# Key factors turned once and spread over all rows by DMA, in a fused Perceiver layer

## The reference, cut to what matters

```python
x2 = layernorm(modality2, ln2_g, ln2_b)
k = x2 @ Wk + bk
scores = jnp.einsum('bqe,bke->bqk', q, k) * scaling
attn = jax.nn.softmax(scores, axis=-1)
```

## Time and profile before

| | us |
|---|---|
| three runs | 562.96, 566.79, 568.53 |
| median | 566.79 |
| the profiled execution | 566.35 |
| its span | 564.6 |
| TensorE busy (matmuls) | 525.6 (93%) |
| VectorE busy | 342.0 (61%) |
| ScalarE busy | 196.1 (35%) |
| GpSimd busy | 193.2 (34%) |
| ScalarE's DMA queue | 17,792 packets, 12.58 MB |
| SP's DMA queue | 24,256 packets, 109.20 MB |

### The profile page before, as it was taken

The page is one execution under the profiler, slowest core; times in us unless marked ns, Lnnn a source line. Parts: engine busy times, 40 slices in busy tenths (PEclk is TensorE's granted clock), DMA queues, the critical chain, the costliest instruction groups (busy, mean ns, idle before and its releaser), DMA issues.

```text
span 564.6 us, 10435 instructions
## 1 busy us (share of the span) xinstructions
PE 525.6 (93%) x4171; PEld 301.9 (53%) x4171; DVE 342.0 (61%) x765; ACT 196.1 (35%) x455; POOL 193.2 (34%) x132
## 2 busy tenths in 40 slices
PE   4979988987999989999998999999988879999996
PEld 2834446553765845666484575656574334444442
DVE  6754185373768468377575836967596895435333
ACT  0233014433723541653373255145143542211110
POOL 0141213224316233440721524269364991000000
PEclk9989999998999999999999999999999989999999
DMA  8999895498499789959959986853527420002002
GB/s 278 424 375 423 330 357 217 184 343 274 174 390 245 276 301 236 324 204 367 262 208 391 202 330 227 241 184 154 113 75 192 145 74 1 1 0 75 0 2 75
DMA packets 42096, 122.45 MB, mean 217 GB/s; under 512 B 19640, under 2 KB 21432, under 8 KB 37312
## 3 DMA queue, kind: packets, MB, share of 16 engines
q1 hardware_dynamic: 24256, 109.20, 53.5%
q10 hardware_dynamic: 17792, 12.58, 9.6%
HBM read 111.29 MB, written 10.49 MB: 216 GB/s over the span
## 4 chain that ended last, share of the span: by engine, by line
PE 61%; DVE 11%; DMA 8%; issue 8%; POOL 5%; ACT 4%; SPq 2%; ACTq 0%; DVEq 0%; POOLq 0%
PE u_ps L914 11%; PE s_ps L1147 9%; PE w_ps L1132 8%; DMA area<-in_kt_dram 6%; PE s_ps L824 6%; PE u_ps L835 5%; PE w_ps L937 5%; POOL area L414 2%; PE w_ps L846 2%; PE w_ps L928 2%; DVE area L1241 2%; PE s_ps L1031 2%; DMA area<-in_nat_dram 2%; PE w_ps L900 1%; DVE area L1325 1%
## 5 line engine op out<-in xcount | busy, mean ns | idle before, releaser
L1241 DVE BATCH_NORM_STATS2 area<-area 128x6 f32<-128x384 f32 (+1 forms) x208 | 99.7, 546 | 26.8 <-DMA area<-in_nat_dram 26.8
L824 PE MATMUL s_ps<-area 128*64 128x512 f32 (+1 forms) x384 | 72.8, 522 | 5.8 <-DMA area<-in_kt_dram 4.8
L914 PE MATMUL u_ps<-area 128*64 128x384 f32 (+1 forms) x416 | 72.4, 491 | 1.2 <-DVE area L1301 1.2
L1147 PE MATMUL s_ps<-area 128*128 128x512 f16 x256 | 61.7, 385 | 4.8 <-DVE area L1520 4.8
L1132 PE MATMUL w_ps<-area 128*128 128x512 f16 x256 | 60.7, 378 | 0.2 <-ACT area L724 0.2
L449 POOL TENSOR_SCALAR area<-area 128x512 f16<-128x512 f32 x32 | 55.6, 1753 | 15.0 <-DMA area<-in_wf_dram 15.0
L414 POOL TENSOR_TENSOR area<-area 128x16 f32<-128x16 f32 (+1 forms) x16 | 39.0, 2438 | 46.6 <-DVE area L1256 46.6
L1283 DVE CUSTOM_DVE_ANT_0 area<-w_ps,area 128x512 f32<-128x512 f32 x24 | 15.4, 690 | 58.6 <-PE w_ps L797 51.8
L724 ACT ACTIVATE area<-w_ps,area 128x512 f32<-128x512 f32 x32 | 22.0, 686 | 79.5 <-PE w_ps L1132 74.0
L824 PEld LDWEIGHTS s_ps<-area 128*64 128x64 f32 x384 | 24.1, 139 | 44.9 <-issue 40.6
L914 PEld LDWEIGHTS u_ps<-area 128*64 128x64 f32 (+1 forms) x416 | 27.6, 135 | 34.2 <-issue 29.5
(11 more groups left out here) (169 smaller groups left out, 835.9 us busy)
## 6 DMA issues: line engine op xcount, KB each, us to landing
area<-in_nat_dram SPq DMA_DIRECT2D x48, 768.0 KB, 10.3
area<-in_kt_dram SPq DMA_DIRECT2D x24, 1536.0 KB, 7.8
area<-in_wf_dram SPq DMA_DIRECT2D x32, 256.0 KB, 8.2
skew<-area ACTq DMA_DIRECT2D x8, 1024.0 KB, 8.6
area<-in_wf_dram SPq DMA_DIRECT2D x16, 512.0 KB, 3.4
area<-in_aw_dram SPq DMA_DIRECT2D x4, 1024.0 KB, 9.3
area<-skew ACTq DMA_DIRECT2D x16, 256.0 KB, 12.2
area<-in_x_dram SPq DMA_DIRECT2D x8, 256.0 KB, 10.2
```

Source lines behind the costliest of these rows:

```text
L824: ins = pe.matmul(S[ch][u * L:(u + 1) * L, 0:n], a_sb[:, c, u * L:(u + 1) * L], x[:, u, c, :], start=(c == 0), stop=(c == KC - 1))
L914: ins = pe.matmul(U[u * L:(u + 1) * L, 0:DC], pT[g % 2][0:m, i, u * L:(u + 1) * L], nat[0:m, j, u, :], start=(j == 0), stop=(j == NJ - 1))
L1147: ins = pe.matmul(S[q], g[i % 3][:, q * P:(q + 1) * P], wf16[:, f, 1, :], start=(f == 0 and z == 0), stop=(f == KF - 1 and z == 1))
L1241: dve.bn_stats(st[b][0:m, 2 * j + u, :], nat[0:m, j, u, :]).then_inc(s["key_stats"], 1)
```

## The change

The factors are no longer spread by ScalarE and turned 13 times. `turn_factors` turns `rs` twice (128 x 13, once for each sequence of the pair) into free columns of `S[3]`; ScalarE copies the 13 x 256 result to SBUF and stores it in DRAM as 26 rows of 128 (13 KB); after a wait for the store it issues two loads, each of which brings one sequence's 13 rows (6,656 B) to 64 partitions. `spread` then holds in SBUF what `W[0]` to `W[2]` and `S[3]` held in PSUM, and `scale_scores` reads it there. `turn_factors(p + 1)` stands ahead of the last chunk of scores, `factors_out` behind `yT_out`, `factors_load` behind the last `scores_out`. `relative(t)` moves ahead of `turn_probs(p, 0)`, and some waits move from `key_factors` to its neighbours. On SP the loads of `wm` move behind those of `nat`, `x` and `kt`.

```diff
+        factor_rows, at = carve(at, [NJ, 2 * P])
...
-        spread, at = carve(at, [P, NJ, P])
+        spread, at = carve(at, [P, NJ * P])
...
+        factors = nc.dram_tensor("factors", (NI, P), F32, kind="Internal").ap()
...
@@ SP, step @@
                 for k in range(NG + 1):
                     if more:
                         load_nat(n + 1, k)
-                    if k in (1, 3, NG) and (1, 3, NG).index(k) + 2 < len(wms):
-                        load_wm(wms[(1, 3, NG).index(k) + 2])
+                for i in wms[2:4]:
+                    load_wm(i)
                 if n + 2 < NT:
                     load_x(n + 2)
                 if more and n:
                     load_kt(n + 1, 2)
-                if len(wms) > 5:
-                    load_wm(wms[5])
+                for i in wms[4:6]:
+                    load_wm(i)
...
@@ ScalarE @@
-            def spread_factors(p, g):
...
+            def factors_out(p):
+
+                act.wait_ge(s["factors_turned"], p + 1)
+                act.copy(factor_rows, S[3][0:NJ, 2 * P:4 * P]).then_inc(s["factors_taken"], 1)
+                act.wait_ge(s["factors_taken"], p + 1)
+                at_least(act, s["factors_spread"], 32 * p)
+                act.dma_start(factors.rearrange("(u j) k -> j u k", u=2), factor_rows.rearrange("j (u k) -> j u k", u=2)).then_inc(s["factors_stored"], 16)
+
+            def factors_load(p):
+
+                act.wait_ge(s["factors_stored"], 16 * (p + 1))
+                at_least(act, s["chunk_scaled"], 4 * p)
+                for u in range(2):
+                    act.dma_start(spread[u * L:(u + 1) * L, :], factors[u * NJ:(u + 1) * NJ, :].rearrange("j k -> (j k)").partition_broadcast(L)).then_inc(
+                        s["factors_spread"], 16)
...
-                if more:
-                    spread_factors(p + 1, 0)
-                    spread_factors(p + 1, 1)
                 if r is not None and more:
                     z_out(r)
...
                 yT_out(p)
                 if more:
+                    factors_out(p + 1)
                     scores_out(p + 1, ORDER[3])
-                    spread_factors(p + 1, 2)
-                    spread_factors(p + 1, 3)
+                    factors_load(p + 1)
                 for i in wms[4:6]:
                     magnitude(i)
...
@@ TensorE @@
-            def key_factors(p):
...
+            def turn_factors(p):
+
+                pe.wait_ge(s["rs_ready"], 2 * (p + 1))
+                pe.wait_ge(s["scores_taken"], 4 * p + PLACE[NCH] + 1)
+                for u in range(2):
+                    ins = pe.transpose(S[3][0:NJ, (2 + u) * P:(3 + u) * P], rs[p % 2].rearrange("p (j u) -> p u j", u=2)[:, u, :], ident_f)
+                ins.then_inc(s["factors_turned"], 1)
...
-            for ch in ORDER:
+            for ch in ORDER[0:3]:
                 scores(0, ch)
+            turn_factors(0)
+            scores(0, ORDER[3])
...
                 if t is not None:
                     q_rows(t)
-                key_factors(p)
                 if n == 0:
                     value_product()
                     value_bias()
                 if t is not None:
                     k_rows(t)
-                turn_probs(p, 0)
                 if t is not None:
                     relative(t)
+                turn_probs(p, 0)
                 turn_probs(p, 1)
...
                 if more:
+                    turn_factors(p + 1)
                     scores(p + 1, ORDER[3])
...
@@ VectorE, scale_scores @@
-                src = W[ch] if ch < NCH else S[3]
-                dve.wait_ge(s["rb_ps"], 4 * p + ch + 1)
+                if ch == 0:
+                    dve.wait_ge(s["factors_spread"], 32 * (p + 1))
                 dve.wait_ge(s["scores_taken"], 4 * p + PLACE[ch] + 1)
-                dve.tensor_tensor_reduce(sc[:, chunk(ch)], src[:, 0:n], sc[:, chunk(ch)], 1.0, -3.0e38, ALU.mult, ALU.max,
+                dve.tensor_tensor_reduce(sc[:, chunk(ch)], spread[:, chunk(ch)], sc[:, chunk(ch)], 1.0, -3.0e38, ALU.mult, ALU.max,
                                          sm(MX + ch)).then_inc(s["chunk_scaled"], 1)
```

More of the change, by code:

```diff
@@ L210, in build_program @@
         names += "xs_stats xs_moments xs_var xs_rstd xs_normed x_turned yTx_out a_ps a_ready cq_terms cq_sum cq_done".split()
-        names += ("key_stats dm_done vs_done d2_done var_ready rs_ready factors_spread rb_ps chunk_scored scores_taken chunk_scaled pair_max "
+        names += ("key_stats dm_done vs_done d2_done var_ready rs_ready factors_turned factors_taken factors_stored factors_spread chunk_scored scores_taken chunk_scaled pair_max "
                   "max_shifted exp_bias_ready exp_done pt_turned pt_taken tile_weighted sums_added reciprocal_ready "
@@ L637, in _ @@
             key_offset_sums(0)
[L638 to L643, removed]
+            scores_out(0, ORDER[1])
+            scores_out(0, ORDER[2])
+            factors_out(0)
+            factors_load(0)
+            scores_out(0, ORDER[3])
             def step(n):
@@ L840, in k_rows @@
                 if t < LAST_T:
-                    pe.wait_ge(s["chunk_scaled"], 4 * (t + 1) + 1)
+                    pe.wait_ge(s["xattn_taken"], t + 1)
                 else:
                     pe.wait_ge(s["att_out_taken"], t - 1)
+                if t == LAST_T - 1:
+                    pe.wait_ge(s["small_step"], 6)
                 for m in range(KD):
@@ L871, in relative @@
                 if t + 1 < NT:
-                    pe.wait_ge(s["chunk_scaled"], 4 * (t + 2))
+                    pe.wait_ge(s["scores_taken"], 4 * (t + 2))
+                    pe.wait_ge(s["factors_taken"], t + 2)
                 if t == 0:
@@ L895, in turn_probs @@
                 pe.wait_ge(s["exp_done"], 3 * p + min(g, 2) + 1)
-                if g >= 2:
+                if g == 0:
+                    at_least(pe, s["yT_taken"], p)
+                    pe.wait_ge(s["a_ready"], KC * (p + 1))
+                elif g == 1:
+                    at_least(pe, s["v_taken"], p - 1)
+                    at_least(pe, s["z_low_ready"], p - 2)
+                    if p == 0:
+                        pe.wait_ge(s["wrow_ready"], 1)
+                else:
                     pe.wait_ge(s["pt_taken"], 4 * p + g - 1)
@@ L1045, in value_bias @@
                 pe.wait_ge(s["sv_ready"], 1)
-                pe.wait_ge(s["chunk_scaled"], 1)
+                pe.wait_ge(s["const_taken"], 2)
                 for e in range(KE):
@@ L1277, in scale_scores @@
             def scale_scores(p, ch):
-                n = CW if ch < NCH else TAIL
-                src = W[ch] if ch < NCH else S[3]
-                dve.wait_ge(s["rb_ps"], 4 * p + ch + 1)
+                if ch == 0:
+                    dve.wait_ge(s["factors_spread"], 32 * (p + 1))
                 dve.wait_ge(s["scores_taken"], 4 * p + PLACE[ch] + 1)
-                dve.tensor_tensor_reduce(sc[:, chunk(ch)], src[:, 0:n], sc[:, chunk(ch)], 1.0, -3.0e38, ALU.mult, ALU.max,
+                dve.tensor_tensor_reduce(sc[:, chunk(ch)], spread[:, chunk(ch)], sc[:, chunk(ch)], 1.0, -3.0e38, ALU.mult, ALU.max,
                                          sm(MX + ch)).then_inc(s["chunk_scaled"], 1)
```

## The result

The changed kernel takes 653.28 us (median of 4 runs, 649.11 to 655.91) against 566.22 for the kernel before (4 runs, 562.96 to 568.53): a ratio of 1.153, 95% interval 1.148 to 1.158. The forecast was 605, at most 636. The profiled execution took 649.11 with a span of 647.2: 82.6 more than the 564.6 of before. Its chain of work that ended last has 12% in the loads of the factors and 5% in their store; neither was there before.

A forecast was written before the change was run, and what follows sets the result against it. TensorE was taken to bound the kernel, busy 44.89 of a 47 us step. Eight boundaries (+1, +3.5, +5.3, four together +24.0, +5.0) add 38.8 to the profiled 566.35: 605 us, range 576 to 636.

The forecast's parts named there:

- the new chain: At each boundary: two turns, factor copy, store, dependent loads, then VectorE's scaling; the weighted sum starts 4.34 us later.
- Each sign that was named: Middle steps: turned probabilities wait 2 to 4 us, loads take 6 to 8, granted clock 0.5, steps 51 to 53.
- 6.94 was forecast from landing to weighted sum: After the factors land, VectorE's scaling and bias, then 4.07 us more until the weighted sum: 6.94 us.
- The second boundary's scores wait: Second boundary: turns ahead of the scores make them wait 3.0 us for factors; loads stay covered; +3.5 us in all.
- the 1.34 that TensorE was to gain: Per boundary, 13 turns become 2: TensorE alone reaches the weighted sum 1.17 us earlier, plus 0.17 of waiting saved.
- The store, 3.0: Boundary, ScalarE's queue: the 13 KB store of the factors lands 3.0 us after issue, with 2.1 and 5 as ends.
- The loads, 7.2: Boundary, ScalarE's queue: both loads, 832 KB, take 7.2 us beside key loads; quiet end 3.5, far end 12.2.
- the two estimates from the Trainium skill: Factor loads: 3.95 us by the page, total 575; 5.9 us at half the rate, total 586.
- The clock, 1.65: After the boundary's idle times of 3.5 and 2.0 us the granted clock falls, adding 1.65 us per boundary.
- The first boundary, +1: First boundary: the 10.53 us value product is extra cover, but the value bias waits for VectorE; 0 to +3, taken +1.
- At the third the last scores: Third boundary: the last scores wait for their keys anyway, hiding the store; +3.6 us, with the clock +5.3.
- The rival with long loads (647): Store at 5 us and loads at 12.2: 7.0 us more at six boundaries, total 647; chance 0.12.

## Why the direction was right and the size wrong

Right, by its own steps: the new chain, its order, and that it ends last. Each sign that was named came, but the sizes were larger: TensorE idles 8.64 at the boundary shown, not 2 to 4, and the step has 58.82, not 51 to 53. At the boundary shown 6.94 was forecast from landing to weighted sum, and 6.90 measured; the two turns take 0.38 (records overlap: 0.31 to the next group, 0.22 forecast), the copy 0.36 (0.38), the scaling from SBUF 0.69 (0.69). The second boundary's scores wait 3.01 for GpSimd (3.0), though its loads (6.36) were not quite covered as forecast: its turns still wait 2.12. SP's order costs little, and of the 1.34 that TensorE was to gain 0.98 came.

Wrong, term by term:

- **The store, 3.0.** This step failed: it was priced by a quiet row and 0.9 on top. It took 4.9 to 5.8 in the first and the third to seventh boundary. At the boundary shown the loads went out 6.08 after the start of the last scores (333.19 to 339.27) where 3.92 was forecast (279.08 to 283.0): 2.16 more. The row that I took, the output's 2.1, came from queues with nothing beside it. I set that against a DMA share of 0.92, and added no more than the 0.9 for it. In the run with few key loads (at most 2.3 to 2.6) and at the eighth boundary (at most 2.50) the store is that short; where it stood, it is not.
- **The loads, 7.2.** 10.07 at this boundary, 2.87 more; 10.0 to 11.7 at the third to eighth. Pricing the loads by the 8.9 of a 1,024 KB store, scaled by bytes, was the failed step with the largest part: with a thirteenth of the bytes the loads still took 5.4 to 6.7, so most of the time does not shrink with them. The scaling took 1.7 off; by the other 1.17 the row itself was short. An estimate from the runs: 3.06 for small loads in the quiet second step, some 3 for the keys beside them and 4.5 with the bytes make 10.6. By the two estimates from the Trainium skill, DMA: Bandwidth & Descriptors, section Anatomy of one DMA and section Queues, rings and completion order (3.95 and 5.9), the loads would be shorter still; the trace has 10.07 at this place.
- **The clock, 1.65.** 2.59 on the first weighted sum alone. I took the price from score matmuls that ran at 0.50 for a part of their time; here nearly all 16 products of the weighted sum ran so. This boundary is the dearest: over the second to eighth it is 1.35 to 2.59, 2.03 in the mean, and not in the order of the idle time ahead (1.47 behind 10.20, 2.58 behind 9.12).
- **The first boundary, +1.** It was +10.5. The prediction counted the value product as cover and named the dot products, but reckoned with short loads, which took 12.96 here, and did not follow ScalarE's queue: `scores_out` behind a load that waits for a store held the product itself. With the dot products ahead of the scaling it is +3.6, so 6.9 are the dot products' and 3.6 the product's.

At the boundary shown the sum closes from the start of the last scores to the weighted sum: 18.06 was forecast (279.08 to 297.14), and 18.06 + 2.16 + 2.87 - 0.04 = 23.05, as measured. The step that ends there grew by 12.03 (58.82 against 46.79): 9.11 on that way, and 2.92 ahead of it, mainly 1.48 in the first weighted sum of the boundary before, at the lower clock, and the 1.20 of waiting for ScalarE. Over all eight, 45 us were missing: 9.5 at the first, 2.3 at the second, 6.0 at the third, 22.4 at the fourth to seventh and 4.8 at the eighth. At the third the last scores (154.95) waited for no keys, so nothing hid the store, where the prediction had counted on that.

The rival with long loads (647) came nearest, 2 below the profiled execution and 6 below the median, with the same mechanism and the far ends of the same two terms (5 and 12.2). That agreement is partly luck: its loads are a little too long, its clock too cheap and its first boundary too small. Its far end came from smaller loads on the same queue, issued elsewhere in the step, some 15 us behind the weighted sum. With 8.9 and 12.2 as the rows of that queue it deserved more than 0.12.

## What to carry to other kernels

A trip through DRAM in the middle of a step is to be priced by what transfers cost at that place, beside the loads that run then, not by its bytes nor by a quiet row; a store and a dependent load pay for the crowd twice, and issuing them 1.2 us sooner into the same crowd did not land them sooner here. On an engine that is busy 95% of the step, 1.3 us of its work is no gain if the replacement is a chain longer than the work that can cover it; the idle time then costs the clock as well (2 us per boundary here). And where a DMA waits for another on a compute engine's queue, everything behind it on that engine waits too (6.54 in the first step), which the profile shows as idle time with no releaser.

## What the runs showed of the hardware

The page's DMA queues of the changed kernel (q1 is SP's, q10 ScalarE's; packets, MB, share of 16 engines):

```profile
q1 hardware_dynamic: 24256, 109.20, 46.8%
q10 hardware_dynamic: 19384, 19.51, 13.8%
```

ScalarE's queue moved 6.93 MB more than before (12.58), and its packets' time rose from 9.6% of 564.6 to 13.8% of 647.2: 54.2 to 89.3 us of all 16 engines, which is 197 GB/s if all of the rise is put down to what was added. The run with short loads has as many packets and 5.51 MB less in 63.9 us (10.3% of 620.6): 217 GB/s for these bytes alone. SP's queue moved its 109.20 MB at 361 (in 302.9 us). The loads with 6,656 B for each of 64 partitions are thus dearer per byte than SP's, about as dear as the queue's other transfers were before (232). Not because they read one row (the run that read 64 different ones has the same time); whether the length of the rows or the 64 partitions is the cause was not tried, nor was a copy without the DRAM between. With fewer key loads the queue's packets took no less time (15.1% of 618.0, 93.3 us), though the loads landed some 3 us sooner: what they lost beside the keys is not in their own packets' time.

A store of 13 KB took 4.9 to 5.8 us beside key loads and at most 2.3 to 2.6 without most of them. And in the run with 32 idle products 1.36 of work between 2.32 and 1.80 of idle did not keep the clock at 1.00, as 0.66 between 1.41 and 1.84 had not in the earlier trace rows.
